# Attention scores from three bf16 parts of queries and keys, with the maximum stream in two-bank slots

## The reference

```python
qkv = x @ W_qkv.T + b_qkv                    # x: layer norm of the stream
q, k, v = jnp.split(qkv, 3, axis=-1)         # 16 heads of 16 features
scores = jnp.einsum('bqhe,bkhe->bhqk', q, k) * scale
scores = jnp.where(causal[None, None], scores, -jnp.inf)
attn = jax.nn.softmax(scores, axis=-1)
out = jnp.einsum('bhqk,bkhe->bqhe', attn, v)
out = out.reshape(b, l, d) @ W_out.T + b_out
```

## Time and profile before

| | us |
|---|---|
| three runs | 1536.26, 1536.66, 1538.86 |
| median | 1536.66 |
| the profiled execution | 1542.46 |
| its span, first to last instruction | 1540.8 |
| PE busy | 1325.7 |
| DVE busy | 1019.6 |
| ACT busy | 775.6 |
| POOL busy | 496.9 |

### The profile page before, as it was taken

The page is one execution under the profiler, slowest core; times in us unless marked ns, Lnnn a source line. Parts: engine busy times, 40 slices in busy tenths (PEclk is TensorE's granted clock), DMA queues, the critical chain, the costliest instruction groups (busy, mean ns, idle before and its releaser), DMA issues. The chain is left out here.

```text
span 1540.8 us, 31184 instructions
## 1 busy us (share of the span) xinstructions
PE 1325.7 (86%) x8678; PEld 1003.7 (65%) x8709; DVE 1019.6 (66%) x2335; ACT 775.6 (50%) x1949; POOL 496.9 (32%) x651
## 2 busy tenths in 40 slices
PE   2628999899699499999998999999778269998998
PEld 1417999799588255555555555554465159997998
DVE  6594555499866777767675777773286755554787
ACT  2524556333244046666675666666546236564333
POOL 1554444255300201222211112212324554443454
PEclk9658999899899569999998999999896569999999
DMA  6503434122465712223322222200315114433233
GB/s 188 169 3 97 123 123 122 60 73 74 146 233 231 136 30 43 44 43 66 61 44 44 43 43 43 44 2 1 114 35 167 55 59 124 123 123 93 83 112 106
DMA packets 86509, 135.73 MB, mean 88 GB/s; under 512 B 12992, under 2 KB 66176, under 8 KB 83328
## 3 DMA queue, kind: packets, MB, share of 16 engines
q1 hardware_dynamic: 64896, 90.29, 22.1%
q0 software_dynamic: 13056, 35.67, 8.3%
q10 hardware_dynamic: 8448, 8.39, 1.6%
HBM read 81.35 MB, written 52.43 MB: 87 GB/s over the span
## 5 line engine op out<-in xcount | busy, mean ns | idle before, releaser
L1448 DVE TENSOR_REDUCE s_MX<-s_ps_a 128x1 f32<-128x512 f32 (+4 forms) x624 | 368.9, 643 | 133.8 <-PE s_ps_a L1515 132.2
L1422 ACT ACTIVATE s_PR<-s_ps_b 128x512 f32<-128x512 f32 (+3 forms) x768 | 343.7, 491 | 162.3 <-PE s_ps_b L1537 155.2
L1515 PE MATMUL s_ps_a<-s_KO,s_QO 96*128 96x512 f32 (+3 forms) x768 | 286.1, 422 | 22.7 <-DMA s_QO<-qk_scratch 22.7
L1537 PE MATMUL s_ps_b<-s_QO,s_KO 98*128 98x512 f32 (+3 forms) x768 | 266.6, 368 | 7.2 <-issue 3.9
L1391 POOL TENSOR_SCALAR_AFFINE_SELECT s_PR<-s_PR 128x256 f32<-128x256 f32 x256 | 103.5, 407 | 474.5 <-ACT s_PR L1422 473.6
L1537 PEld LDWEIGHTS s_ps_b<-s_QO,s_KO 98*128 98x128 f32 x768 | 146.3, 194 | 72.6 <-ACT s_PR L1422 54.4
L603 POOL DMA_INDIRECT f_XG<-xn_scratch,f_tok_u x144 | 136.4, 947 | 167.3 <-PE f_ps_x L700 157.4
L1515 PEld LDWEIGHTS s_ps_a<-s_KO,s_QO 96*128 96x128 f32 x768 | 152.1, 211 | 28.7 <-DVE s_MX L1448 20.8
L810 POOL DMA_INDIRECT f_YG<-y_scratch,f_slots_u x128 | 121.0, 945 | 150.2 <-DVE X L885 94.6
L1552 PE MATMUL s_ps_o<-s_PR,s_VG 128*17 128x512 f32 (+3 forms) x1536 | 163.0, 496 | 5.3 <-POOL s_PR L1391 5.3
L656 DVE TENSOR_TENSOR f_xl<-f_ps_x,f_xh 128x256 fp32r<-128x256 f32 x144 | 61.1, 425 | 97.7 <-ACT f_xh L628 92.6
(11 more groups left out here) (206 smaller groups left out, 2966.9 us busy)
## 6 DMA issues: line engine op xcount, KB each, us to landing
y_scratch<-f_YS SPq DMA_DIRECT2D x144, 128.0 KB
s_KO<-qk_scratch SPq DMA_DIRECT2D x48, 256.0 KB, 5.8
s_QO<-qk_scratch SPq DMA_DIRECT2D x96, 128.0 KB, 6.6
xn_scratch<-f_XN ACTq DMA_DIRECT2D x16, 512.0 KB, 3.2
qk_scratch<-p_QKh SPq DMA_DIRECT2D x32, 256.0 KB
qk_scratch<-p_QKl SPq DMA_DIRECT2D x32, 256.0 KB
f_stage<-in_w_up SPq DMA_DIRECT2D x20, 352.0 KB
X<-in_x SPq DMA_DIRECT2D x4, 1024.0 KB, 9.4
```

Of the source, the lines that this page charges most:

```text
L1422: nc.scalar.activation(PR[:, u // 2 % SLOTS, u % 2, 0:W - lo], ps_b[u % RING][:, lo:W], ACT.Exp, scale=SCALE).then_inc(exp_done, 1)
L1448: nc.vector.tensor_reduce(MX[:, h:h + heads, i, s], ps_a[v % RING][:, 0:heads * keys].rearrange("p (h n) -> p h n", h=heads), AX.X, ALU.ma ...
L1515: last = nc.tensor.matmul(ps_a[v % RING][:, at:at + keys], QO[k][0:R, h, i * P:(i + 1) * P], KO[k][0:R, h % 2, s * W:s * W + keys], start= ...
L1537: nc.tensor.matmul(ps_b[u % RING][:, lo:W], KO[k][0:RM, h % 2, i * P:(i + 1) * P], QO[k][0:RM, h, hf * W + lo:(hf + 1) * W], start=True, s ...
```

## The change

In `project_stage` each number becomes the sum of three bf16 parts. ACT writes the first (`part1`), DVE the rest in fp32 (`REST`, two buffers), ACT the second part (`part_2`, one step later), POOL the third (rest minus second). One DMA per step writes all three, in pieces of 1 KB, where there were two DMAs in pieces of 2 KB.

In `softmax_stage` the six products (0,0), (0,1), (1,0), (1,1), (0,2), (2,0) of parts fill the same 96 rows, 16 each. Queries and keys have all four heads side by side, so no zeros are written, and 12 DMAs per group load them instead of 9, of the same total size. The memsets of ones (`KO`, now 3 rows of 4096 bf16 elements) no longer stand before the loads. The maximum becomes three bf16 rows: ACT makes the first, DVE the rest, POOL two more instructions (`max_rest`, ahead of its masks of step 8), and three DMAs place them.

PSUM is divided anew: `ps_a` has two slots of two banks. A unit of stream a is now filled for two heads at once, one in each bank, and read by one DVE instruction over both banks: 21 units per group (`AHEAD` is 7) instead of 39. The banks are masked one by one, so there are 26 mask matmuls per group instead of 23, with the same 4,096 columns. `ps_t` is gone: the transposed output and the transposed maximum each take one slot in turn with the units, in an order (`USES`) that PE and DVE share, and one semaphore, `slot_read`, counts the slots read. A slot is filled only after the use two before it was read. `turn_output` and `turn_max` now stand behind the second b-matmul of their steps (1, 7 and 8) instead of behind `pv_step`; DVE reads the first unit of a step, then the output or the maximum, then the other units.

The core of the diff:

```diff
 project_stage
-                sp.wait_ge(qkh_done, n + 1)
-                sp.dma_start(qk_dram[w // 2, g, 0, :, cols], QKh[:, g, :].bitcast(F32)).then_inc(qk_out[g], 16)
-                sp.wait_ge(qkl_done, n + 1)
-                sp.dma_start(qk_dram[w // 2, g, 1, :, cols], QKl[:, g, :].bitcast(F32)).then_inc(qk_out[g], 16)
+                sp.wait_ge(part3_done, n + 1)
+                sp.dma_start(qk_dram[w // 2, g, :, :, cols].rearrange("t p l -> p t l"),
+                             QK[:, g, :, :]).then_inc(qk_out[g], 16)
...
+            for n in range(NW * G):
+                pool.wait_ge(part2_done, n + 1)
+                nc.gpsimd.tensor_tensor(QK[:, n % G, 2, :], REST[:, n % 2, :], QK[:, n % G, 1, :],
+                                        ALU.subtract).then_inc(part3_done, 1)
...
+            def part_2(n, g):
+                act.wait_ge(rest_done, n + 1)
+                nc.scalar.activation(QK[:, g, 1, :], REST[:, g % 2, :], ACT.Copy).then_inc(part2_done, 1)
...
 softmax_stage
+    PAIRS = ((0, 0), (0, 1), (1, 0), (1, 1), (0, 2), (2, 0))
+    R = len(PAIRS) * HD
+    RM = R + PARTS
...
-            wide = W // keys
-            starts = range(0, GH, wide)
-            A_UNITS += [(i, s, h, min(wide, GH - h), keys) for h in starts]
+            wide = min(W // keys, 2)
+            A_UNITS += [(i, s, hp, wide, keys) for hp in range(0, 2, wide)]
...
-        ps_a = [ps(f"ps_a{i}", [P, W]) for i in range(RING)]
+        ps_a = [ps(f"ps_a{i}", [P, 2, W]) for i in range(2)]
...
-        ps_t = ps("ps_t", [P, W])
...
             for g in range(4):
-                sp.wait_ge(zeros[g % 2], g // 2 + 1)
-                sp.wait_ge(ones, g + 1)
                 load(g)
...
+            def max_rest(g):
+                pool.wait_ge(slot_read, max_slot(g)[0] + 1)
+                nc.gpsimd.tensor_copy(NMS[:, 1, :], NMR[:, :]).then_inc(max2_done, 1)
+                pool.wait_ge(max2_done, g + 1)
+                nc.gpsimd.tensor_tensor(NMS[:, 2, :], NMR[:, :], NMS[:, 1, :], ALU.subtract).then_inc(max3_done, 1)
...
-                    nc.vector.tensor_reduce(MX[:, h:h + heads, i, s],
-                                            ps_a[v % RING][:, 0:heads * keys].rearrange("p (h n) -> p h n", h=heads),
-                                            AX.X, ALU.max).then_inc(a_read, 1)
+                    _, slot = slot_of_a(g, v)
+                    scores = ps_a[slot][:, :, 0:heads * keys].rearrange("p c (h n) -> p c h n", h=heads)
+                    nc.vector.tensor_reduce(MX[:, hp:hp + heads, :, i, s].rearrange("p h c -> p c h"), scores, AX.X,
+                                            ALU.max).then_inc(slot_read, 1)
...
-                    if v >= RING or since(g, 1):
-                        pe.wait_ge(a_read, NA * g + v + 1 - RING)
+                    if not isinstance(g, int) or q >= 2:
+                        pe.wait_ge(slot_read, q - 1)
...
-                        if h == GH - 1:
-                            if n >= 1:
-                                pv_step(g, k, n - 1)
+                        if h == 1:
                             if n == 1 and since(g, 1):
                                 turn_output(g - 1, 1)
-                            if n == MAX_T - 1:
+                            if n == OUT_T:
                                 turn_output(g, 0)
                             if n == MAX_T and until(g, 1, NG):
                                 turn_max(g + 1)
+                        if h == GH - 1 and n >= 1:
+                            pv_step(g, k, n - 1)
```

More of the change, by code:

```diff
@@ L1493, in _ @@
                         max_low(g + 1)
+                    for groups, v in A_BESIDE[n][1:]:
+                        a_beside(g, groups, v)
             normalise(NG - 1, 3, 1)
@@ L1500, in a_units @@
                 for v in units:
[L1501 removed]
+                    i, s, hp0, heads, keys = A_UNITS[v]
                     diagonal = s == i // 4
+                    q, slot = slot_of_a(g, v)
+                    banks = [ps_a[slot][:, c, :] for c in range(2)]
                     if v == 0:
                         pe.wait_ge(operands[k], LOAD * (quarter(g, k) + 1))
[L1505 to L1506 removed]
+                    if not isinstance(g, int) or q >= 2:
+                        pe.wait_ge(slot_read, q - 1)
@@ new lines, in a_units @@
+                    for hp in range(hp0, hp0 + heads):
+                        at = (hp - hp0) * keys
+                        for c in range(2):
+                            h = 2 * hp + c
+                            last = nc.tensor.matmul(banks[c][:, at:at + keys], QO[k][0:R, h, i * P:(i + 1) * P],
+                                                    KO[k][0:R, h, s * W:s * W + keys], start=not diagonal,
+                                                    stop=True, skip_group_check=True)
```

221 lines of the change are left out of this document (121 added, 100 removed).

## The result

The changed kernel takes 1550.42 us (median of 4, 1548.34 to 1551.12) where the kernel before takes 1536.46: a ratio of 1.0086, 95% interval 1.0068 to 1.0103. On a second chip it was 1.0044 (1.0026 to 1.0062). So it is slower, by 7 to 14 us. The forecast was +23.5, 1560 us: the sign was right, and the time lies within the range and just inside the forecast's 1549 to 1572, but the sum came out 10 us too high (16 by the second chip). Its terms were off by more than that, in both directions, so that the total came as near as it did is in part luck.

The account below looks back on a forecast made before the run. The prediction took PE's instruction stream as the bound. Per group -3.6 + 5.6 = +2.0 us; fourteen groups +28, the last two -1.5, the start -3: +23.5, or 1560 us on the median, range 1530 to 1584.

Parts of the forecast that it names:

- (a) Streams: PE's score products: a 512-column bf16 product takes 0.215 us instead of 0.235, saving 1.4 us per group.
- (b) Masks and small products: PE's masks in bf16 save 1.1 us per group, the eight 128-column products of stream a 0.45.
- (c) The exit of a value step: The weight load exposed behind each of 12 value steps is halved, saving 0.75 us per group.
- The saving, 3.6: PE's total saving per group from streams, masks, small products and value-step exits: 3.7 us, used as 3.6.
- The waits, +5.6: Walking a group's program order: PE's added waits on slots, and for ACT at narrow steps, cost 5.6 us per group.
- together 2.1: Steps 0 and 1 of a group: PE waits 0.77, 0.73 and 0.63 us for slots, together 2.1.
- Start of the stage: Softmax stage's start: loads issued earlier without zeros, DVE writing ones first; 3 us gained, bounds -1 and 6.
- Projection: ACT's extra activation and POOL's subtraction fit within each 2.1 us step: 0, with 2 us at the projection's end.
- The clock falls as well: Rival, chance 0.16: PE's waits bring one 1.2 GHz spell per group, +18 us in all, time 1578.
- It doesn't do what it says: Rival, chance 0.08: bf16 streams and weights are no faster in this mix; +4 us per group, time 1588.
- The slots are deep enough: Rival, chance 0.13: a gain if slot waits stay below 3.6 us per group; 1521 with half, 1495 with none.
- What would show it: Signs of being wrong: a group under 33.7 us, 1.2 GHz spells inside groups, or the stage's loads the first wait again.

Follow-up runs that it names:

- combined: ring_bf16 with the first maximum's transfers ahead of later loads, POOL's two instructions behind step 8's masks, and ones written by POOL: 1485.65 us, ratio 0.9644.
- ring_bf16: The changed kernel with its bf16 scores, but the maximum stream back in three one-bank buffers and transposes in their own bank: 1507.07 us, ratio 0.9819.
- slots_fp32: The kernel before with the two slots of two banks alone, parts still 4-byte and transposes in the slots: 1582.25 us, ratio 1.0317.

## Why the prediction was right or wrong, point by point

**What bounds the kernel** held for the kernel before: PE's stream, with DVE and ACT at two thirds. In after PE stands still for a tenth of a group, mostly for DVE's readings.

**(a) Streams** held: in after, a 512-column bf16 product starts 0.215 to 0.220 us after the one before it where the 4-byte ones stood 0.235 apart, 384 columns 0.163, 256 columns 0.110. The Trainium skill, page "TensorE: Matmul & The Clock Gate", section "Back-to-back issue gap", which the prediction quotes, calls its 216 ns the gap of an isolated product, names no type, and gives 131 ns for a stream. The bf16 stream here keeps to the 216, the 4-byte one does not, and no row shows 131.

**(b) Masks and small products** held: a masked product's mask takes 0.058, and a 128-column product 0.055.

**(c) The exit of a value step** was mis-sized. From the value step to the product behind it it is 0.525 us as before, so the 0.75 of this term never came.

**The saving, 3.6**: without the slots (combined) a group is 33.74 - 30.84 = 2.9 shorter. That is about 3.6 less term (c), but not the saving alone: PE waits 0.6 us for DVE in step 1 there. PE's own busy time in a group falls by 3.3 in combined and by 2.5 in after.

**The waits, +5.6**: the places were right, the price was not. Against combined, after is 0.59 and 0.50 longer at steps 0 and 1 (2.1 forecast), 1.16 at step 7 (1.3), 0.88 and 0.76 at steps 8 and 9 (1.85), -0.2 at steps 4 to 6 (+0.3), and nothing for ACT at the narrow steps (0.7): 3.7 us. The term that was most off is "together 2.1". The three waits are 1.75 long in the trace, and faster products meet DVE at the same place in the ring too: step 1 takes 3.64 in combined and 3.28 before, with stream a's products 0.60 apart, the pace of one reading. In combined:

```profile
738.15 0.33 PE L1557 MATMUL s_ps_b<-s_QO,s_KO 99*128 99x384 bf16 x1
738.52 0.10 PEld L1533 LDWEIGHTS s_ps_a<-s_KO,s_QO 96*128 96x128 bf16 x1 [0.42 <-DVE s_MX L1464]
738.52 0.39 PE L1533 MATMUL s_ps_a<-s_KO,s_QO 96*128 96x512 bf16 x1
...
739.12 0.39 PE L1533 MATMUL s_ps_a<-s_KO,s_QO 96*128 96x512 bf16 x1
```

From 738.15 to 738.52 is 0.37 where 0.163 would do, a wait of 0.2, three times: 0.6. The slots cost 1.75 - 0.6, the 1.1 of the step table. The walk set the slots' waits against those of the kernel before, not against those of a bf16 kernel without the slots. Steps 8 and 9 need one more word: combined also has POOL's instructions behind the masks, which in the ring is worth 1.0 at step 9. Against ring_bf16, which has them ahead as after does, the slots cost 2.7 and not 3.7.

**Net per group**: +2.0 forecast, +0.5 to +0.9 measured in eleven of the fourteen groups. The fourteen together, group 0 and the back edge with them, are 9.3 us longer where 28 were forecast, 19 too much.

**The last two groups**: -1.5 forecast, -5.7 measured. Part of it is that before had two spells at 1.2 GHz in the last group and after has none; slots_fp32 and ring_bf16 take 30.8 and 29.8 us for this group, against 32.9 before and 27.6 after. The rest was not separated. In the sum the groups and these two came out 23 us too high, and start and projection 10 too low: the errors half cancel.

**Start of the stage**: 3 us gained was forecast, 6.5 lost. Three steps failed. The loads do go out 4 us earlier behind the projection, but their data takes 15.6 us for 12, so PE begins at the same place, and its first wait is again the loads:

```profile
521.41 0.59 PE L1568 MATMUL s_ps_a<-s_neg,s_identb 128*128 128x256 bf16 x2 [22.30 <-DMA s_KO<-qk_scratch]
```

DVE's memsets of ones go by elements (3.47 us for 3 x 4096 bf16), the slow end of the bounds; the Trainium skill, page "VectorE: DVE Perf Modes", section "Zero memsets can be issued as uint32", says so (one cycle per element whatever the type), and the trace agrees: the same 3.47 us stand before for 4096 elements of 4 bytes. And of the third row for the maximum "it has 3 us of cover" is true inside the stage only: at its start all rows stand behind 48 loads. I had read the time to the first load's landing and not the rate of the queue. The later start is partly paid back in group 0 (-2.5), since the clock rises 8 us after the group's first product before (at 562.7 us), and 3 us after it in after (at 565.2).

**Projection**: 0 forecast, +2.2 measured (from the first product, which stands at 416.8 us before, not at 423, to the last). At its end, from the last product to the issue of the last write, it is +2.1, 2 forecast. The step "neither has more than the step" counted ACT and POOL alone. DVE's normalisation takes twice its time whenever POOL's subtraction runs beside it: 0.88 us, where most of those ahead of the first subtraction take 0.41. In most steps DVE's record starts 0.43 us behind POOL's and ends 0.15 us behind POOL's end, as if it waited for it. Before, and after with POOL, over 430 to 490:

```profile
L1134 DVE TENSOR_SCALAR p_XN<-X,MV,p_RSTD 128x256 f32 (+1 forms) x25 | 10.2, 406 | 0.0
```

```profile
L1086 POOL TENSOR_TENSOR p_QK<-p_REST,p_QK 128x512 bf16<-128x512 f32 x25 | 29.3, 1171 | 31.0 <-ACT p_QK L1107 31.0
...
L1147 DVE TENSOR_SCALAR p_XN<-X,MV,p_RSTD 128x256 f32 (+1 forms) x24 | 21.0, 877 | 0.0
```

DVE is then busy for 68.6 of 83.9 us (56.8 of 81.7 before), and PE's transposes stand behind it: their weight loads are idle for DVE six times, 1.9 us together, and PE itself for 0.7 (425 to 495 us; before has none of either in this stretch). The Trainium skill, page "GPSIMD Engine Reference", section "1. Specifications", names this: the ports are shared with VectorE, with contention for instructions in a 2-port mode (whether the normalisation ran in one no trace shows). The readings of PSUM and the two-operand instructions kept their time here (0.75 and 0.41 us). No run took POOL's subtraction away, so the tie is the overlap in the trace, not an experiment.

**The rivals.** "The clock falls as well": not in the way that was meant. Groups 1 to 6 and 9 to 13 of after are at full clock throughout, although PE stands still for a tenth of each; group 0 has the clock's rise, and groups 7 and 8 a longer time at 1.2 GHz behind the back edge than before has (13 us for 10). "It doesn't do what it says": no; streams and weight loads are faster. "The slots are deep enough": the point of decision was right (a gain if the waits stay below the saving), and they exceeded it by 0.8 us a group. One figure there does not follow from the prediction's own terms: with no waits -3.6 per group gives 1482, not 1495. In the same way waits of 4.5 to 6.5 give 1546 to 1574, a little wider than the 1549 to 1572 of the forecast.

**What would show it.** Readings of 1024 columns take 1.22 us, bf16 products stand 0.215 apart, and the weight loads of stream a wait for DVE for some 5 us of each group, as foretold. A group is 34.5 us, below the 35 to 36.5 that was named. And one of the three signs of being wrong came true: the stage's loads are the first wait again.

## What to carry to other kernels

Do not count a ring of buffers by its bytes alone. Here two slots of two banks, shared with the transposes, cost 2.7 to 3.4 us a group more than three of one bank and a bank for the transposes, although the reader had less to do in total; halving the readings gave nearly all of it back. Cost a two-part change as two kernels, each part alone, and set a new wait against the kernel that has the gain already. And ask of every first use in a stage what is queued ahead of it on its DMA queue, and how fast that queue runs: moving three small transfers brought the stage's first exponentials 6 us earlier.

## What was not expected of the hardware

- Loads that all go to 16 partitions move at 118 to 130 GB/s here, with loads to 16 and 32 partitions in turn it is 164 to 175; a copy whose slowest source dimension has two elements moves at 52.
- DVE's fp32 scale-and-shift from SBUF takes 0.88 us instead of 0.41 while POOL subtracts.
- The loop's back edge costs 6.0 us once in combined. PE stands still for 4.1 us (3.9 before); the granted clock falls during that stop and stays at 1.2 GHz for 6.8 us in combined, 10 before and 13 in after. Before:

```profile
831.39 0.79 PE L1537 MATMUL s_ps_b<-s_QO,s_KO 98*128 98x512 f32 x1 [3.93 <-issue]
```
